# Own term, array halves and shorter attention sums in a graph network kernel on one Trainium2 core

## The reference

```python
# 1: two gin layers
h = agg + x                       # agg: sum of x[src] over the edges of each dst
h = relu(h @ W_a + b_a)           # 32 -> 64 in the first layer
out = h @ W_b + b_b               # 64 -> 64, then 64 -> 32 in the second
# 2: twice, on x = relu(x), with own loops added once more
x = segment_sum(x[src] * dinv[src] * dinv[dst], dst)
# 3: three spline convolutions with batch norm
agg = segment_sum(basis-weighted z[src], dst) / count;  x = agg + x @ R + b
# 4: attention with 4 heads
att = softmax over the edges of a node of leaky_relu(a_src + a_dst + fc_b)
out = mean over heads of segment_sum(att * (x @ w)[dst], src) + bias
```

## Time and profile before

| what | us |
|---|---|
| median of 3 runs | 11817.92 (11816.22 to 11818.46) |
| the profiled execution's own time | 11816.44 |
| its span in the profile | 11814.7 |

### The profile page before, as it was taken

The page is one execution under the profiler, slowest core; times in us unless marked ns, Lnnn a source line. Parts: engine busy times, 40 slices in busy tenths (PEclk is TensorE's granted clock), DMA queues, the critical chain, the costliest instruction groups (busy, mean ns, idle before and its releaser), DMA issues.

```text
span 11814.7 us, 183469 instructions
## 1 busy us (share of the span) xinstructions
PE 7462.7 (63%) x56926; PEld 5697.7 (48%) x56926; DVE 6685.9 (57%) x18825; ACT 1846.8 (16%) x1630; POOL 8104.9 (69%) x8392
## 2 busy tenths in 40 slices
PE   7999897877666666667666666666666500321325
PEld 4675676767445554445445454555455400321324
DVE  9996212122666666666666666666666601553557
ACT  6996000000111111111111111111111000000000
POOL 6541776776677777757777775777777477777771
PEclk8998998999788888878888887878877755765767
DMA  3442665887100000010000001000000021221221
GB/s 110 139 146 101 192 194 169 293 261 256 17 13 13 13 13 13 13 16 13 13 13 13 13 13 16 13 13 13 13 13 13 10 44 32 62 53 40 62 51 38
DMA packets 654764, 750.92 MB, mean 64 GB/s; under 512 B 264009, under 2 KB 393499, under 8 KB 654165
## 3 DMA queue, kind: packets, MB, share of 16 engines
q10 hardware_dynamic: 202256, 401.00, 10.3%
q0 software_dynamic: 264960, 153.69, 8.5%
q1 hardware_dynamic: 187078, 190.14, 5.3%
HBM read 568.54 MB, written 175.70 MB: 63 GB/s over the span
## 4 chain that ended last, share of the span: by engine, by line
POOL 51%; issue 19%; PE 16%; DVE 4%; DMA 0%; DVEq 0%; ACT 0%; SPq 0%; POOLq 0%; ACTq 0%
POOL work L877 51%; PE ps L1083 6%; PE ps L1067 2%; PE ps L1068 1%; PE ps L1070 1%; PE ps L987 1%; PE ps L1117 1%; PE ps L1132 1%; PE ps L1066 1%; PE ps L1154 1%; PE ps L1237 1%; PE ps L1248 0%; PE ps L1213 0%; PE ps L1265 0%; DVE nodes L1729 0%
## 5 line engine op out<-in xcount | busy, mean ns | idle before, releaser
L877 POOL DMA_INDIRECT work<-tab_sp,nodes x4983 | 4716.0, 946 | 1721.4 <-issue 1517.0
L1132 PE MATMUL ps<-work 128*128 128x192 f32 x9984 | 2663.8, 411 | 1909.5 <-DVE work L1797 1847.6
L1132 PEld LDWEIGHTS ps<-work 128*128 128x128 f32 x9984 | 1986.0, 231 | 2485.7 <-issue 1438.0
L2050 DVE TENSOR_TENSOR work<-work,ps 128x192 f32 x4992 | 1745.9, 350 | 726.4 <-PE ps L1132 383.0
L877 POOL DMA_INDIRECT work<-tab_att,nodes x1661 | 1602.2, 965 | 629.6 <-issue 629.6
L1117 PE MATMUL ps<-work,wk 128*32 128x144 f32 x10080 | 1758.6, 327 | 2.3 <-DVE work L2050 2.3
L1797 DVE TENSOR_TENSOR work<-work,ps 128x512 f32<-128x512 f32 x1248 | 855.6, 686 | 1318.3 <-DMA work<-tab_sp,nodes 1292.1
L1450 ACT ACTIVATE work<-zero 128x2496 f32<-128x2496 f32 x318 | 725.4, 2282 | 5446.0 <-PE ps L1117 5441.4
L1117 PEld LDWEIGHTS ps<-work,wk 128*32 128x32 f32 x10080 | 1144.7, 124 | 558.0 <-issue 363.0
L2038 DVE TENSOR_TENSOR work<-work,ps 128x384 f32<-128x384 f32 x2496 | 1364.7, 547 | 0.0
L1882 DVE TENSOR_TENSOR big<-big,ps 32x12 f32 (+2 forms) x1600 | 248.3, 155 | 1262.0 <-PE ps L987 1046.4
(11 more groups left out here) (292 smaller groups left out, 8295.6 us busy)
## 6 DMA issues: line engine op xcount, KB each, us to landing
nodes<-counts_d ACTq DMA_DIRECT2D x648, 550.0 KB
counts_d<-nodes SPq DMA_DIRECT2D x50, 2475.0 KB
work<-tab_sp,nodes POOLq DMA_INDIRECT x4983, 2.4
work<-edge_rows SPq DMA_DIRECT2D x112, 320.0 KB
edge_rows<-work ACTq DMA_DIRECT2D x104, 320.0 KB, 2.2
work<-tab_att,nodes POOLq DMA_INDIRECT x1661
work<-tab_gcn,nodes POOLq DMA_INDIRECT x698
work<-tab_h,idx POOLq DMA_INDIRECT x509
```

What stands on the lines that cost most here:

```text
L877: pool.indirect_dma_start(out=rows(p, r)[:, t, 0:ROW[p]], out_offset=None, in_=TABLE[p], in_offset=bass.IndirectOffsetOnAxis(ap=place, axi ...
L1132: last = nc.tensor.matmul(moment_place(t), u0[:, s % 2, t % SUB, :], vb[:, t % AHEAD, :, :].rearrange("p k j -> p (k j)"), start=True, sto ...
L2050: v.tensor_tensor(to, to, got, ALU.add).then_inc(mom_added.sem, 1)
```

## The change

**Own term.** In the close way the features are no longer turned for gcn1 and gcn2: all of `acc` is cleared by one memset per block, PE's node phase multiplies each tile of sums with `ident4` (the 32 by 32 identity four times, 128 rows and 32 columns), which sums the four groups, and DVE adds the nodes' own features from `tb`, where they lie. ACT's count loads now wait only for the piece's last use in the pass before. The attribute load on SP waits for the end of gcn2's node phase.

**Array halves.** In gin1 and gin2 the two column ranges of the hidden product go to partitions 0 to 63 and 64 to 127, so to two column halves of the array; weights and biases are loaded twice (`w2`, `w4`, `b1c`, `b3c`: four more loads on ACT's queue). The relu of a block is two instructions, of 384 columns on 128 partitions and of 128 on 64. The second product reads its two parts from the two row halves. DVE adds gin2's bias in two operations.

**Attention sums.** A one-hot covers 48 nodes (QW) instead of 144; each group of four tiles has its own first node, and its own sum of 48 columns in the same bank. DVE adds the four sums of a half one after the other, each waiting for the one before, at first nodes read by a load of eight registers for two halves. The places are counted from every fourth tile's first node (`quarter_first`, loaded with a stride of 4, 416 values to each of 128 partitions). At the setup DVE checks with three more operations that four tiles span fewer than 48 nodes; if not, the other way is taken.

The diff, cut to its core:

```diff
...
@@ -337,6 +338,8 @@
+        quarter_span = firsts_of[32:33, 0:ET // SUB].bitcast(F32)
+        most_span = sb("most_span", [1, 1])
...
@@ -397,7 +400,7 @@
-        places = ps[:, 7, 0:GW]
+        places = ps[:, 7, 0:QW]
...
@@ -730,8 +734,8 @@
-                sp.dma_start(xc_flat[:, ET:ET + HALVES].bitcast(I32),
-                             half_base.broadcast_to([P, HALVES])).then_inc(near_in, 16)
+                sp.dma_start(quarter_first, dst_base.rearrange("o (s q) -> o s q", q=SUB)[:, :, 0].broadcast_to([P, ET // SUB]),
+                             allow_slow_non_contiguous=True).then_inc(near_in, 16)
@@ -756,7 +760,7 @@
-                        sp.wait_ge(parts_ready, len(UNITS))
+                        sp.wait_ge(out_done.sem, out_done.done(p, BLOCKS - 1))
@@ -849,9 +853,7 @@
-                            pool.memset(acc[C:2 * C, cols], 0.0)
-                            pool.memset(acc[2 * C:3 * C, cols], 0.0)
-                            pool.memset(acc[3 * C:P, cols], 0.0).then_inc(acc_clear, 1)
+                            pool.memset(acc[:, cols], 0.0).then_inc(acc_clear, 1)
@@ -1146,13 +1148,13 @@
-                        hold(pe, "pe", agg_added.sem, agg_added.done(p, k - 2))
+                        hold(pe, "pe", agg_added.sem, agg_added.done(p, SUBS * (k - 2) + (SUBS - 1)))
...
-                            last = nc.tensor.matmul(ps[:, 4 + h, 0:GW], weighed[:, s, t % SUB, :], near_half[:, h, t, :],
-                                                    start=(t == 0), stop=(t == G - 1))
+                            last = nc.tensor.matmul(ps[:, 4 + h, s * QW:(s + 1) * QW], weighed[:, s, t % SUB, :], near_half[:, h, t, :],
+                                                    start=(t % SUB == 0), stop=(t % SUB == SUB - 1))
@@ -1230,11 +1232,11 @@
-                    hold(pe, "pe", hid_ready.sem, hid_ready.done(p, b - (1 if p == "gin1" else 2)))
-                    weight, bank = (w1, 0) if p == "gin1" else (w3, 2 * (b % 2))
+                    hold(pe, "pe", hid_ready.sem, hid_ready.done(p, b - 2))
+                    weight = w1 if p == "gin1" else w3
...
-                    for c0, c1 in block_halves:
-                        last = nc.tensor.matmul(flat(bank, BN, HID)[:, c0:c1], weight[0:kk, :],
+                    for side, (c0, c1) in enumerate(block_halves):
+                        last = nc.tensor.matmul(ps[side * HID:(side + 1) * HID, b % 2, 0:c1 - c0], weight[0:kk, :],
@@ -1244,13 +1246,14 @@
-                        for c0, c1 in block_halves:
-                            last = nc.tensor.matmul(flat(2, BN, HID)[:, c0:c1], w2[:, :], hid[0:HID, b % 2, c0:c1],
+                        for side, (c0, c1) in enumerate(block_halves):
+                            rows_ = slice(side * HID, (side + 1) * HID)
+                            last = nc.tensor.matmul(ps[0:HID, 2 + side, 0:c1 - c0], w2[rows_, :], hid[rows_, b % 2, 0:c1 - c0],
...
-                    hold(pe, "pe", out_done.sem, out_done.done(p, b - 4))
+                    hold(pe, "pe", out_done.sem, out_done.done(p, b - (2 if p == "gin2" else 4)))
@@ -1260,13 +1263,15 @@
-                            last = nc.tensor.matmul(to(C), hid[0:HID, b % 2, j * P:(j + 1) * P], w4[:, :], start=True, stop=True)
+                            side, at_ = divmod(j, SUB)
+                            rows_ = slice(side * HID, (side + 1) * HID)
+                            last = nc.tensor.matmul(ps[:, 4 + 2 * (b % 2) + side, at_ * C:(at_ + 1) * C],
+                                                    hid[rows_, b % 2, at_ * P:(at_ + 1) * P], w4[rows_, :],
+                                                    start=True, stop=True)
...
-                            w = P
-                            parts = ps[:, 2 * (b % 4) + j // SUB, (j % SUB) * w:(j % SUB + 1) * w]
-                            last = nc.tensor.transpose(parts, tile(w, b, j), ident[0:w, 0:w])
+                            last = nc.tensor.matmul(to(C), tile(P, b, j), ident4[:, :], start=True, stop=True)
...
@@ -1380,11 +1385,12 @@
-                    bank = 0 if p == "gin1" else 2 * (b % 2)
...
-                    nc.scalar.activation(hid[0:HID, b % 2, :], flat(bank, BN, HID), ACT.Relu,
-                                         bias=bias[:, :]).then_inc(hid_ready.sem, 1)
+                    both = BN - SUB * P
+                    nc.scalar.activation(hid[:, b % 2, 0:both], ps[:, b % 2, 0:both], ACT.Relu, bias=bias[:, :])
+                    nc.scalar.activation(hid[0:HID, b % 2, both:SUB * P], ps[0:HID, b % 2, both:SUB * P], ACT.Relu,
+                                         bias=bias[0:HID, :]).then_inc(hid_ready.sem, 1)
@@ -1429,9 +1435,11 @@
+                before = 0 if p == "gin2" else UNITS[LINEAR[LINEAR.index(p) - 1]] * NCH
...
-                    hold(act, "act", piece_used.sem, piece_used.done(p, c - PIECES))
+                    last_here = c - PIECES if c >= PIECES or not before else -1 - (before - 1 - r) % PIECES
+                    hold(act, "act", piece_used.sem, piece_used.done(p, last_here))
@@ -1554,9 +1562,10 @@
-                    turn(LINEAR[LINEAR.index(p) - 1])
...
+                    else:
+                        turn(LINEAR[LINEAR.index(p) - 1])
@@ -1716,18 +1725,19 @@
-                        v.tensor_tensor(yn[:, tiles, :], got, b4r[:, :].unsqueeze(1).broadcast_to([P, BT, C]),
-                                        ALU.add).then_inc(out_done.sem, 1)
+                        for side, n in ((0, SUB), (1, BT - SUB)):
+                            t0 = b * BT + side * SUB
+                            got = ps[:, 4 + 2 * (b % 2) + side, 0:n * C].rearrange("p (t c) -> p t c", c=C)
+                            ins = v.tensor_tensor(yn[:, t0:t0 + n, :], got, b4r[:, :].unsqueeze(1).broadcast_to([P, n, C]),
+                                                  ALU.add)
+                        ins.then_inc(out_done.sem, 1)
...
-                        for t0, n in ((0, SUB), (SUB, BT - SUB)):
-                            parts = ps[:, 2 * (b % 4) + t0 // SUB, 0:n * P].rearrange("p (t q c) -> p t c q", q=QT, c=C)
-                            ins = v.tensor_reduce(dst[:, b * BT + t0:b * BT + t0 + n, :], parts, axis=AX.X, op=ALU.add)
-                        ins.then_inc(out_done.sem, 1)
+                        v.tensor_tensor(dst[:, tiles, :], got, tb[:, tiles, :], ALU.add).then_inc(out_done.sem, 1)
@@ -2102,31 +2112,37 @@
-                first_of = xc_flat[:, ET:ET + HALVES].bitcast(I32)
-                by_half = (lambda a: a.rearrange("p (k t) -> p k t", t=G))
+                by_quarter = (lambda a: a.rearrange("p (k t) -> p k t", t=SUB))
...
-                link(v.tensor_tensor(by_half(xc_flat[:, 0:ET]), by_half(near),
-                                     first_of.unsqueeze(2).broadcast_to([P, HALVES, G]), ALU.subtract))
+                link(v.tensor_tensor(by_quarter(xc_flat[:, 0:ET]), by_quarter(near),
+                                     quarter_first.unsqueeze(2).broadcast_to([P, ET // SUB, SUB]), ALU.subtract))
...
-                link(v.tensor_copy(places, iota_f[:, :]))
+                link(v.tensor_copy(places, iota_f[:, 0:QW]))
...
-                def add_half(j, h, to_node):
+                def add_half(j, h, to_nodes):
...
-                    dve.wait_ge(agg_added.sem, agg_added.done(p, m - 1))
-                    to = acc[:, bass.ds(to_node, GW)]
-                    v.tensor_tensor(to, to, ps[:, 4 + h, 0:GW], ALU.add).then_inc(agg_added.sem, 1)
+                    for s in range(SUBS):
+                        dve.wait_ge(agg_added.sem, agg_added.done(p, SUBS * m + (s - 1)))
+                        to = acc[:, bass.ds(to_nodes[s], QW)]
+                        v.tensor_tensor(to, to, ps[:, 4 + h, s * QW:(s + 1) * QW], ALU.add).then_inc(agg_added.sem, 1)
+
+                def firsts_of_halves(j):
+                    by_sub = base[0:1, bass.ds((j + first) * G, 2 * G)].rearrange("o (s q) -> o s q", q=SUB)
+                    dve.load(regs[0:2 * SUBS], by_sub[:, :, 0])
+                    got = [dve.snap(r, min_val=0, max_val=N) for r in regs[0:2 * SUBS]]
+                    return got[0:SUBS], got[SUBS:]
...
-                    v.tensor_tensor(near_half[:, h, :, :], places.unsqueeze(1).broadcast_to([P, G, GW]),
-                                    xc_flat[:, bass.ds((j + first) * G, G)].unsqueeze(2).broadcast_to([P, G, GW]),
+                    v.tensor_tensor(near_half[:, h, :, :], places.unsqueeze(1).broadcast_to([P, G, QW]),
+                                    xc_flat[:, bass.ds((j + first) * G, G)].unsqueeze(2).broadcast_to([P, G, QW]),
@@ -2140,13 +2156,11 @@
-                    dve.load(regs[0:2], half_prev[0:1, bass.ds(2 * i + (first + 1), 2)])
-                    to_nodes = [dve.snap(r, min_val=0, max_val=N) for r in regs[0:2]]
+                    to_nodes = firsts_of_halves(2 * i)
...
-                dve.load(regs[0:2], half_prev[0:1, first + n - 1:first + n + 1])
```

(12 more changed lines are left out.)

32 lines of the change are left out of this document (17 added, 15 removed).

## The result

| | before | after |
|---|---|---|
| median of 7 runs, us | 11817.82 (11816.22 to 11823.24) | 11852.53 (11834.43 to 11882.79) |
| profiled execution, us | 11816.44 | 11852.53 |
| its span, us | 11814.7 | 11850.8 |

What follows compares the result with a forecast made beforehand. GpSimd's row gathers were taken as half the span; edited stages were priced by PE's busy time and clock. Terms summed to +34 on 11816.4, with the median 1.5 higher: 11852 us, range 11780 to 11885, the forecast's own 11836 to 11868.

Steps and rivals of the forecast that it cites:

- Attention sums: Attention: PE at 1.2 GHz becomes the bound, 6.8 us a half; chunk 3 +31, chunk 4 +28, node phase after +4 us.
- The rival of the full clock: Attention sums: PE reaches 2.4 GHz, DVE stays the bound at about 4.8 us a half; 11781 us in all; chance 0.30.
- the faster case: Whole kernel: below 11794 us, mainly full clock in the attention sums with a warm gin1; chance 0.21.
- Own term: gcn1 and gcn2: each node phase +16 us; earlier gathers give -4 us in gcn1 and -10.6 us in gcn2.
- gin1: First node phase: array halves overlap products and the clock rises after two or three blocks, -42 us.
- gin2: Second node phase: hidden product 2/7 shorter at a clock of 1.00 over 14 blocks, -6 us.
- The loose ends: Strided near load hidden, 90 to 280 us without cover; three more DVE operations at the setup, +1.5 us.

Runs made afterwards that it cites:

- e1: Kernel before with only the attention sums over 48 nodes and the setup check: 11882.82 us, ratio 1.0054.
- e5: Changed kernel with each matmul of the attention sums moving the same 48 columns three times: 11814.18 us, ratio 0.9994 to the kernel before.
- e6: Kernel before with array halves in gin1 alone, gin2's node phase as before: 11783.32 us, ratio 0.9963.
- e3: Kernel before with only the array halves, in gin1 and gin2: 11779.85 us, ratio 0.9970.
- e4: Changed kernel with the attention sums as they were, own term and array halves kept: 11811.17 us, ratio 0.9986 to the kernel before.
- e7: Kernel before with 48 unread PE transposes in the wait of gin1's first block: 11805.88 us, ratio 0.9984.
- e9: Changed kernel with the moving operand repeated in sums, own term and attention's node phase, and first nodes side by side for the register load: 11758.66 us, ratio 0.9938 to before.

## Why the prediction was right, and where it was not

*Attention sums: right, by its mechanism.* The step said that PE begins each chunk at 0.50, mostly loads and so stays there, 6.8 us a half. It did (6.84), e1 showed the cost by itself, and e5 that the clock rises when the same loads stand beside three times the columns, so the few columns that move keep it down. (24 x 6.8 + 3 is 166 and not 167, and 84 / 16 is 5.25; neither matters.) The rival of the full clock was wrong about the clock here. In the Trainium skill, "TensorE: Matmul & The Clock Gate", Part 1, sustained activity releases the clock. By that a PE that is busy for 108.0 of 108.0 us would not stand at 0.50; the trace disagrees.

*And that rival's price was wrong too.* Its 4.8 us a half and 11781 took at most 1.10 us for the register load, from a load of 16. With a distance between the values, 8 take 1.84 us and hold DVE up for 2.6. With the clock up a half takes 5.8 to 6.0 us (e5), more than the 5.25 of before. So the faster case was never there for the change as it is.

*Own term: right in each of its four terms*, within 2 us each: phases of 42 us at the cold price of the nearest form, the stall gone, the store 3 us slower under the count loads, the memsets out of the way.

*gin1: right in direction, mis-sized.* The step had 5/7 of a product's time, 5.9 us for a cold block and 3.75 for a warm one. Measured from one start to the next, a product takes 0.60 of its time: cold 1.89 us (gin2's after, from 1841.28) where 3.18 stood before (gin1's, from 1102.68; the 3.3 of the forecast is the busy time of rows that overlap a little), and at 1.00 the 0.99 us of the second pair of rows here, from gin1 after, where the first pair, from gin2 before, has 1.64:

```profile
1892.33 1.72 PE L1237 MATMUL ps<-big,w 128*64 128x512 f32 x4
1893.97 0.29 PE L1263 MATMUL ps<-w,work 64*128 64x32 f32 x1
...
1101.50 1.07 PE L1251 MATMUL ps<-work,w 64*64 64x512 f32 x4
1102.49 1.07 PE L1239 MATMUL ps<-big,w 97*64 97x512 f32 x4
```

With the 384 columns wholly beside the 512 it would be 1024 of 1792 columns, 4/7 or 0.57, so nearly all of them are hidden, on row halves (L1251) as on column halves. Blocks take 4.8 us cold (e6) and 3.0 warm; in the warm ones PE waits for ScalarE. What was not seen is that the moment at which the clock rises differs from run to run: after two blocks in the changed kernel's profiled execution, five in e3's, nine or so in e4's, never in e6's. The term lies between -34 and -55 us in these. e6, with this part alone, spreads over 22 us and e3, with gin2's halves too, over 37, so this is a good part of the 48; what makes up the rest no profile shows.

*gin2: wrong in sign.* The step kept the clock of 1.00 and took 6 us off (2/7 of 1.8 us, fourteen times, is 7.2). The clock fell within 6 us of the phase's start and stayed down, and the phase took 7.4 us more. e6, with gin2's products as they were, got the clock back. That the shorter product leaves the 32-column passes more of each block would explain it, but this is argued, not shown. The sum came out within 1 us because gin1's extra 13 and gin2's missing 13 cancel. That is luck, and so is the median within 1 us when the runs spread over 48: the own range of the forecast, 11836 to 11868, holds only three of the seven.

*The loose ends: right in the setup and right that the load is hidden, wrong in one price.* The setup took 1.9 us more, where 1.5 stood. The strided load took 40.3 us to land and DVE waited 39.0 for it, where 90 to 280 stood as its price without cover. It cost nothing: from the attention's table store to DVE's first softmax weights there are 505 us in both kernels (9447.80 to 9952.8 and 9422.64 to 9927.4). In the tile's rows:

```profile
  DMA xc<-in_dst_base: 39.0, 1
...
DMA to landing us min/median/max: 4.0/7.4/40.3
```

The queue's line in the profile shows the packets, 240,198 (in e1 too) where there were 187,078:

```profile
q1 hardware_dynamic: 240198, 190.30, 5.7%
```

In the Trainium skill, "DMA: Bandwidth & Descriptors", Rules for kernel authors, a strided last dimension becomes one descriptor per element. The 53,120 packets more agree with the 53,248 elements.

## What to carry to other kernels

Before PE is given smaller pieces, look for a phase of the same form in the trace and read its granted clock: here a pass with 32 columns on a 128 by 128 stationary operand took 0.213 us where one with 128 took 0.112, and one with 48 took 0.214 where one with 144 took 0.143 (e5). Where PE stands still before a phase that then runs cold, work that nobody reads can pay (18 us in the median of e7, 37 in its fastest run), and repeating the moving operand cost nothing here, where PSUM had room. And read a sum that comes out right by its terms: two of these were off by 13 us in opposite directions.

## What the runs showed of the hardware

- Repeating the moving operand: a pass with 128 columns took 0.112 us at 1.00 (e9), a pass with 32 columns 0.213 us at 0.50 and 0.111 before its clock fell. So moving four times the columns cost nothing, and in the attention's node phase of e9 the clock stayed up.
- Two f32 products on halves of the array overlap nearly wholly, on column halves and on row halves: the four passes of a block's product take 0.60 of their time in single file, 1.89 us for 3.18 at 0.50 and 0.99 for 1.64 at 1.00.
- The same phase got its clock back after 2, 5, some 9 blocks or not at all, in different executions of like code. Why it differs stays open.
- A register load of 8 values at a distance of four took 1.84 us, of 8 side by side 0.60 (e9), of 16 side by side 1.10.
